# Delta-rule recurrence on one core: the leaf decays on GpSimd, the last leaf written into the compact array, and WL's product ahead of the identity's

## What is computed

```python
def step(S, t):
    q_t, k_t, v_t, a_t, b_t = t
    y = jnp.einsum('bhvk,bhk->bhv', S, k_t)
    err = y - v_t
    S = a_t[..., None] * S - (b_t[..., None] * err)[..., None] * k_t[:, :, None, :]
    o = jnp.einsum('bhvk,bhk->bhv', S, q_t)
    return (S, o)
```

## Time and profile before

| | |
|---|---|
| median of 3 runs | 3173.81 us (3172.24 to 3183.9) |
| profiled execution | 3174.62 us, of which the span 3172.8 us |
| TensorE busy | 2838.1 us, 89% |
| VectorE busy | 2322.8 us, 73% |
| ScalarE busy | 1605.5 us, 51% |
| GpSimd busy | 1317.6 us, 42% |
| granted TensorE clock, mean | 0.977 of full speed |

### The profile page before, as it was taken

How to read it: one execution, slowest core, us unless ns; L and a number is a source line. 1 busy time by engine, 2 the same in 40 slices (tenths; PEclk the granted TensorE clock), 3 DMA queues, 4 the chain that set the end, 5 groups by cost and what they waited for, 6 DMA issues and landing times. The chain is left out here.

```text
span 3172.8 us, 48588 instructions
## 1 busy us (share of the span) xinstructions
PE 2838.1 (89%) x14144; PEld 2012.0 (63%) x14144; DVE 2322.8 (73%) x4837; ACT 1605.5 (51%) x3516; POOL 1317.6 (42%) x1574
## 2 busy tenths in 40 slices
PE   7999999678898898988989898898888989869999
PEld 3555555366676776666766676776767767645555
DVE  6777777578888778887787878788887788724332
ACT  6666666445555555554554555555555555421111
POOL 3666767624443444443443434444334444310000
PEclk9999999889999999999999999999999999979999
DMA  3655565631222322222323222322223222034220
GB/s 133 242 202 231 234 241 202 225 60 34 54 42 41 60 51 54 43 41 42 69 41 55 41 42 43 67 46 51 42 41 65 46 54 42 8 105 89 55 44 14
DMA packets 449884, 261.23 MB, mean 82 GB/s; under 512 B 402672, under 2 KB 414672, under 8 KB 447472
## 3 DMA queue, kind: packets, MB, share of 16 engines
q1 hardware_dynamic: 449664, 258.51, 31.5%
HBM read 153.42 MB, written 105.05 MB: 81 GB/s over the span
## 5 line engine op out<-in xcount | busy, mean ns | idle before, releaser
L265 DVE SCALAR_TENSOR_TENSOR A_acc<-A_psY,A_w,A_acc 128x410 f32<-128x410 f32 (+1 forms) x720 | 419.2, 637 | 151.6 <-ACT A_acc L334 151.6
L1155 ACT ACTIVATE B_WL<-B_psT 64x128 f32<-64x128 f32 (+3 forms) x480 | 148.6, 310 | 512.4 <-PE B_psT L1576 512.4
L840 POOL TENSOR_TENSOR B_WT<-B_WT,B_G 128x128 f32<-128x128 f32 (+2 forms) x224 | 183.0, 817 | 513.0 <-PE B_psT L1576 493.3
L405 PE MATMUL A_psY<-A_xT,A_w 128*128 128x413 f32 (+1 forms) x960 | 347.2, 510 | 9.1 <-PE A_psAG L411 7.7
L192 POOL TENSOR_TENSOR A_outs<-A_outs,A_acc 128x410 f32<-128x410 f32 (+1 forms) x240 | 229.7, 987 | 215.5 <-ACT A_outs L342 215.5
L1068 DVE TENSOR_TENSOR B_NC<-B_NC,B_psM 128x256 f32<-128x256 f32 x480 | 199.1, 415 | 143.9 <-PE B_psM L1603 101.8
L405 PEld LDWEIGHTS A_psY<-A_xT,A_w 128*128 128x128 f32 x960 | 180.2, 189 | 165.5 <-issue 164.2
L822 POOL TENSOR_TENSOR B_PQ<-B_PQ,B_G 128x256 f32<-128x256 f32 x128 | 125.8, 983 | 368.3 <-DVE B_WT L1036 368.3
L1071 DVE TENSOR_REDUCE B_W<-B_NC 128x64 f32<-128x320 f32 x512 | 248.7, 486 | 17.6
L1603 PE MATMUL B_psM<-B_BD,B_WL 128*128 128x128 f32 x1536 | 237.6, 296 | 12.6
L334 ACT ACTIVATE A_acc<-A_psY,A_w 128x410 f32<-128x410 f32 (+1 forms) x240 | 166.2, 692 | 162.9 <-PE A_psY L405 161.2
(11 more groups left out here) (197 smaller groups left out, 6703.5 us busy)
## 6 DMA issues: line engine op xcount, KB each, us to landing
B_KQ<-scr SPq DMA_DIRECT2D x96, 512.0 KB, 6.8
scr<-A_outs SPq DMA_DIRECT2D x48, 615.0 KB, 3.5
scr<-A_outag SPq DMA_DIRECT2D x32, 615.0 KB, 5.2
scr<-A_outs SPq DMA_DIRECT2D x48, 409.0 KB, 2.5
A_xc<-nbeta SPq DMA_DIRECT2D x16, 1024.0 KB, 5.9
B_A<-scr SPq DMA_DIRECT2D x32, 512.0 KB, 5.0
B_C<-scr SPq DMA_DIRECT2D x32, 512.0 KB, 5.9
B_G<-scr SPq DMA_DIRECT2D x32, 512.0 KB, 4.6
```

The lines of the kernel that those rows point to most:

```text
L265: nc.vector.scalar_tensor_tensor(a, y, w[:, s, col:col + 1], a, ALU.mult, ALU.add)\
L405: last = nc.tensor.matmul(psY[p][:, y0:y0 + HALO + t1 - t0], wp[:, p, kt, :], xT[:, kt, t0:t1 + HALO], start=kt == 0, stop=kt == KT - 1)
L840: tt(dst, dst, gr, ALU.mult).then_inc(wsc.sem, 1)
L1155: copy = lambda out, in_: nc.scalar.activation(out, in_, ACT.Copy)
```

## The change

Three edits, all in the recurrence.

1. In leaves 3, 7 and 11 VectorE writes the decayed W of the last leaf into its place in WC instead of WT. TensorE waits for the first copy alone. ScalarE copies that leaf from WC back to WT after the WL copy, and `scale_left` on GpSimd waits for this.
2. The decays of chunk g + 1 are six GpSimd products of one row each (`row_decays`, 128x256), spread over leaves 2 to 9: part 0 after the first two gates, part 1 in leaf 4, part 2 after leaf 6's right scaling, part 3 after leaf 7's left scaling, parts 4 and 5 in leaves 8 and 9. `dec` counts 6 instead of 3. Chunk 0's stay on VectorE.
3. In even leaves but leaf 0 TensorE issues the WL product first (`start=True`) and the identity product second.

```diff
-DEC = 3
+DEC = 6
...
+            def row_decays(g, *parts):
+
+                a, e = by_leaf_row(A[:, g % 2]), E[:, g % 2]
+                products = ((RR_, a[:, 1], a[:, 2]), (B_, e[:, RR_], a[:, 3]), (F_ + 1, a[:, 0], a[:, 1]),
+                            (B_ + 1, a[:, 2], a[:, 3]), (F_ + 2, e[:, F_ + 1], a[:, 2]), (F_ + 3, e[:, F_ + 2], a[:, 3]))
+                for k in parts:
+                    row, x, y = products[k]
+                    if k == 0:
+                        loaded(pool, "A", g)
+                        wait(pool, nc0, 2 * g - 3, 5)
+                    else:
+                        wait(pool, dec, g, {1: 1, 4: 3, 5: 5}.get(k, 0))
+                    tt(e[:, row], x, y, ALU.mult).then_inc(dec.sem, 1)
...
                 wait(pool, tps, g, j + 1)
+                if p >= 2:
+                    wait(pool, wc, g, {3: 2, 7: 4, 11: 6}[j])
...
                 gates(0, 1)
+                rows(0)
                 past(g, 3)
...
                 gates(3)
+                rows(1)
                 past(g, 5)
...
                 scale_right(g, 7, (1,))
+                rows(2)
                 past(g, 7)
                 scale_left(g, 7)
+                rows(3)
                 past(g, 8)
                 scale_right(g, 9)
+                rows(4)
                 past(g, 9)
                 scale_left(g, 9)
+                rows(5)
                 scale_right(g, 11)
...
-                    tt(WT[:, j] if j % 2 else WR[:], W[:, :, lf], E[:, g % 2, B_:B_ + R, :, j].rearrange("p r h -> p h r"), ALU.mult).then_inc(wt.sem, 1)
+                    p, n, _ = merge_of(j)
+                    if j < JM and p >= 2:
+                        to = WC[:, 0:H * n].rearrange("p (h t) -> p h t", h=H)[:, :, n - R:n]
+                    else:
+                        to = WT[:, j] if j % 2 else WR[:]
+                    tt(to, W[:, :, lf], E[:, g % 2, B_:B_ + R, :, j].rearrange("p r h -> p h r"), ALU.mult).then_inc(wt.sem, 1)
...
-                    elif j == 8 and more:
-                        decays(g + 1, (0,))
...
-                            decays(g + 1, (1,))
...
-                            wait(act, wt, g, j + 1)
-                            left_compact(g, j, (j,))
                         wait(act, tps, g, j + 1)
                         wait(act, mps, g, 2 * j)
...
                         copy(WL[0:rows_, 0:w_], psT[0:rows_, 0:w_]).then_inc(wl.sem, 1)
+                        if p >= 2:
+                            wait(act, wt, g, j + 1)
+                            copy(WT[:, j], WC[:, 0:H * n].rearrange("p (h t) -> p h t", h=H)[:, :, n - R:n]).then_inc(wc.sem, 1)
...
-                            wait(pe, wc, g, {3: 2, 7: 4, 11: 6}[j])
+                            wait(pe, wc, g, {3: 1, 7: 3, 11: 5}[j])
...
-                            wait(pe, psc0, g, pair_number(j) + 1)
-                            mm(psM[:, 0:2 * rs], ident[:], pair(g)[:, :, :, r0:r0 + n], start=True, stop=False)
-                            wait(pe, wl, g, j + 1)
-                            mm(psM[:, 0:2 * rs], WL[0:rs, 0:128], OWN[0:rs, j // 2, :, :, R:2 * R],
-                               start=False, stop=True).then_inc(mps.sem, 2)
+                            if j:
+                                wait(pe, wl, g, j + 1)
+                                mm(psM[:, 0:2 * rs], WL[0:rs, 0:128], OWN[0:rs, j // 2, :, :, R:2 * R], start=True, stop=False)
+                                wait(pe, psc0, g, pair_number(j) + 1)
+                                mm(psM[:, 0:2 * rs], ident[:], pair(g)[:, :, :, r0:r0 + n],
+                                   start=False, stop=True).then_inc(mps.sem, 2)
```

More of the change, by code:

```diff
@@ L578, in recurrence @@
         kl, kc = Count(sem("leaf_keys"), 2), Count(sem("block_keys"), 3)
-        wc = Count(sem("left_compact"), 6)
+        wc = Count(sem("left_rearranged"), 6)
         wec = Count(sem("w_end"), 2)
@@ L852, in _ @@
                 queries(1)
+                rows = lambda *parts: row_decays(g + 1, *parts) if g + 1 < NCH else None
                 past(g, 2)
                 gates(0, 1)
+                rows(0)
                 past(g, 3)
@@ L904, in _, with first_decays @@
             wait(dve, zeros, 0, NZERO)
[L906 to L921, removed]
+            def first_decays():
+                loaded(dve, "A", 0)
+                wait(dve, dcp, 0, 2)
+                a, e = by_leaf_row(A[:, 0]), E[:, 0]
+                tt(e[:, F_ + 1:B_ + 2:3], a[:, 0:3], a[:, 1:4], ALU.mult).then_inc(dec.sem, 3)
+                wait(dve, dec, 0, 3)
+                tt(e[:, F_ + 2:B_ + 1:4], e[:, F_ + 1:RR_ + 1:3], a[:, 2:4], ALU.mult).then_inc(dec.sem, 2)
+                wait(dve, dec, 0, 5)
+                tt(e[:, F_ + 3], e[:, F_ + 2], a[:, 3], ALU.mult).then_inc(dec.sem, 1)
             def coefs(h):
@@ L1134, in chunk @@
                     add_state(g, i)
-            decays(0)
+            first_decays()
             nc.vector.memset(NC[:, 1], 0.0).then_inc(zeros.sem, 1)
@@ L1341, in chunk @@
                         p, n, r0 = merge_of(j)
-                        if p >= 2:
-                            wait(act, wt, g, j + 1)
-                            left_compact(g, j, (j,))
                         wait(act, tps, g, j + 1)
@@ L1584, in chunk @@
                             wait(pe, ow, g, 2 if j < 8 else 4)
-                            wait(pe, psc0, g, pair_number(j) + 1)
-                            mm(psM[:, 0:2 * rs], ident[:], pair(g)[:, :, :, r0:r0 + n], start=True, stop=False)
-                            wait(pe, wl, g, j + 1)
-                            mm(psM[:, 0:2 * rs], WL[0:rs, 0:128], OWN[0:rs, j // 2, :, :, R:2 * R],
-                               start=False, stop=True).then_inc(mps.sem, 2)
+                            if j:
[4 more added lines that the diff above has]
+                                   start=False, stop=True).then_inc(mps.sem, 2)
+                            else:
+                                wait(pe, psc0, g, 1)
+                                mm(psM[:, 0:2 * rs], ident[:], pair(g)[:, :, :, r0:r0 + n], start=True, stop=False)
+                                wait(pe, wl, g, 1)
+                                mm(psM[:, 0:2 * rs], WL[0:rs, 0:128], OWN[0:rs, 0, :, :, R:2 * R],
+                                   start=False, stop=True).then_inc(mps.sem, 2)
                         else:
```

## The result

The changed kernel takes 3118.65 us (median of 4 runs, 3117.38 to 3120.34) against 3174.42 for the one before (4 runs): ratio 0.9819, interval 0.9804 to 0.9834. I had predicted 3177, with 3140 to 3200 as the range. The profiled execution took 3120.34 us.

A forecast was written before the change was run, and what follows sets the result against it. VectorE and TensorE were taken to end the recurrence's leaves in turn. Gains and costs nearly cancelled, +0.1 us a chunk, +3 us over 31 chunks: 3177 us as a median, range 3140 to 3200.

The forecast's parts named there:

- The ring: Each leaf's loop through VectorE, TensorE and ScalarE back to VectorE; VectorE and TensorE were said to take turns ending it.
- Decays onto GpSimd: Six 128x256 products, 6.0 us on GpSimd, covered there; VectorE sheds 3.42 us a chunk but waits in collisions.
- I take 0.80 us each, 1.6 us: Leaves 6 and 7: parts 2 and 3 each delay a VectorE solution step by 0.80 us, bounded by 0 and 1.13.
- Rival C: Leaves 6 and 7: a full block, parts 2 and 3 costing 1.13 us each, 3197 us; chance 0.07.
- Leaf 10's transposition comes forward by its idle 1.11 us and no more: Leaf 10 on TensorE: VectorE's relief gains only the 1.11 us idle there, 1.1 us a chunk if nothing else happens.
- Part 5 against the decayed W: Leaf 10: part 5 pushes two scalings onto the decayed W, 0.4 us of VectorE, hidden on TensorE's side.
- Part 0 at leaf 3 and part 4 at leaf 9: Each can hold up that leaf's decayed W on VectorE while TensorE is still busy; counted as 0.
- The compact route: Leaves 3, 7, 11: ScalarE's copy leaves the way, gaining 0.24 us at leaf 3, 0.33 at 11, nothing at 7.
- The later left scaling: GpSimd's left scaling comes about 0.5 us later, with no user for several leaves; 0.5 cost if that cover were gone.
- The swap: WL product first in even leaves: costs 0.39 us at leaves 4 and 12, gains up to 0.35 at leaf 8.
- rival B: Slower by the product order: TensorE also ends leaves 2 and 6, 0.78 us a chunk more, 3201 us; chance 0.17.
- A: Parts 2 and 3 slip into VectorE's gaps and the relief is gained: -1.1 us a chunk, 3140 us; chance 0.36.

The follow-up runs named there:

- compact_only: The kernel before with only the last leaf (3, 7, 11) written straight into the compact array: 3155.75 us, ratio 0.9927.
- decays_only: The kernel before with only the next chunk's decays moved from VectorE to GpSimd: 3158.79 us, ratio 0.9923.
- no_swap: The changed kernel with the old order, identity product ahead of the WL product: 3140.84 us, ratio 0.9889 against the kernel before.
- swap_only: The kernel before with only the WL product put ahead of the identity product in even leaves but leaf 0: 3217.35 us, ratio 1.0126.
- row2_moved: The changed kernel with decay row product 2 made right after row product 1, away from leaf 6's solution steps: 3107.77 us, ratio 0.9796 against the kernel before.
- fill_before: The kernel before with leaf 9's second decay transposes issued three times to fill TensorE's idle time, same output: 3189.95 us, ratio 1.005.
- fill_before_swap14: The kernel before with leaf 9's second decay transposes issued three times and the WL product first in leaf 14 alone: 3159.43 us, ratio 0.9942.

## Why the prediction was wrong, step by step

The ring, leaf by leaf: by how much the stretch between two products grew against the kernel before, as the sum had it and as even chunks show it (medians of chunks 2 to 30), in us.

| from product of leaf | predicted | measured | off by |
|---|---|---|---|
| 0 to 6 | +0.15 | -0.03 | -0.18 |
| 6 to 7 | +0.80 | +0.36 | -0.44 |
| 7 to 8 | +0.80 | +0.43 | -0.37 |
| 8 to 9 | -0.91 | -0.80 | +0.11 |
| 9 to 10 | -1.14 | -1.56 | -0.42 |
| 10 to 11 | +0.40 | +0.17 | -0.23 |
| 11 to 12 | -0.30 | -0.30 | 0 |
| 12 to 14 | +0.40 | +0.25 | -0.15 |
| 14 to the next chunk | -0.20 | +0.01 | +0.21 |
| sum | 0 | -1.47 | -1.47 |

**Decays onto GpSimd: the mechanism right, the term mis-sized.** The step that failed is "I take 0.80 us each, 1.6 us". The products met the two solution steps named. Leaf 7's product came 0.36 later, leaf 8's another 0.43, 0.79 together, and of this the decays are 0.71: `compact_only`, which moves no decays, already shows 0.07 at leaf 8. There were two reasons. The rows are cheaper than 1.13: parts 2 and 3 took 0.91 and 1.04 us even while contended (part 2 alone 0.68). The nearest row that I took, 1.13, has another access pattern; the six parts come in two kinds, 0.66 us with both inputs from A and 0.86 with one from E, when they meet nothing. And the price was carried over from products that begin under a VectorE instruction in full course. Part 2 starts at 1512.33 while the step before it (1511.41 for 1.42 us) is nearly through; the step it holds up appears at 1512.68, when the product has 0.56 us left to its end at 1513.24, and it lost 0.40. Part 3 had 0.49 left when the last step of leaf 7 appeared at 1518.44, which lost 0.35. In both, then, the loss was a little less than what was left of the GpSimd product when the step appeared (that the rest at that moment is what counts is my reading of these two cases). The second collision made leaf 8's product late, but not the leaf: TensorE was busy until about 1520.6 and stood still 0.1 us before the transposition of 1520.72. This is read from the rows; no run moved part 3 alone.

Put right by the 0.81 us of the two rows in the table, the sum would have been about 3153 us, inside the range. It took the next step and the clock as well to bring the result below it.

The Trainium skill's page "SBUF — State Buffer" (section "SBUF: two separate sides") describes the shared port pair as an exclusive lock held for the whole instruction, with the loser fully blocked. The runs agree on the exclusion: the step took 1.27 us with part 2 beside it and 0.87 without. By a lock over the whole instruction a loser waits at most the winner's length; here it waited 0.40 of 0.91 us, since 0.35 of them were over when it began. Rival C, which priced the full block, had no support.

**"Leaf 10's transposition comes forward by its idle 1.11 us and no more": true, and not the bound.** Counted from leaf 0's product it came forward 1.01 us in the odd chunks shown (from 38.20 to 37.19) and 1.13 in the medians. The product of leaf 11 came forward more, 1.30 and 1.42, because TensorE had not been what ended that leaf. Two engines' timelines of the kernel before:

```profile
1554.13 0.49 PE L1588 MATMUL B_psM<-B_OWN,B_WL 64*128 64x128 f32 x2
```

```profile
1552.73 0.27 DVE L1073 TENSOR_TENSOR B_WR<-B_W,B_E 128x64 f32<-128x64 f32 x1
...
1553.30 0.29 DVE L1031 TENSOR_TENSOR B_PQ<-B_PQ,B_E 128x128 f32<-128x128 f32 x1
...
1554.25 1.27 DVE L1012 TENSOR_TENSOR B_ST<-B_ST,B_ring 128x512 f32<-128x512 f32 x2
...
1555.44 0.41 DVE L1068 TENSOR_TENSOR B_NC<-B_NC,B_psM 128x256 f32<-128x256 f32 x1
```

The merged term was there at 1554.62, and the product waited 0.8 us more for VectorE's own queue. VectorE had no idle time from leaf 9 to leaf 11, and in the changed kernel none from leaf 10's product to leaf 11's. So leaf 11's product follows leaf 10's, which came forward 1.61, less 0.19 that part 5 adds. I had read TensorE's idle time before its own instruction as the limit, where the question was which engine releases the next product last. A smaller part of the same step: I let leaf 10's product wait for the modelled end of the matmuls before it, while it starts 0.19 us ahead of that end (1525.16 against 1524.64 + 0.71).

**Part 5 against the decayed W.** Predicted 0.4 us of VectorE, hidden behind TensorE. L1095 took 0.37 instead of 0.27 and the scaling behind it, L1048, 0.36 instead of 0.29. With the small shifts between them that makes 0.19, and it is not hidden: VectorE releases leaf 11's product, which is 0.18 further from leaf 10's in `decays_only` too. Part 0 at leaf 3 and part 4 at leaf 9 cost nothing, as put.

**The compact route.** By `no_swap` against `decays_only`: 0.25 gained at leaf 4 (predicted 0.24), nothing gained at leaf 7, as put, and 0.3 at leaf 12 (0.3). The swap in the changed kernel cancels the first. The later left scaling, which I had put at nothing, cost 0.07: it now meets a step of leaf 7's solution that takes 1.50 us instead of 1.43, in `compact_only` as well.

**The swap.** By the changed kernel against `no_swap`: leaf 5 is 0.42 later (predicted 0.39), of which 0.19 comes back before leaf 6's product, where I had carried all of it on; between leaves 8 and 9 it gains 0.33 (predicted up to 0.35); between 9 and 10 another 0.20, not predicted; between 12 and 13 it loses 0.25 (predicted 0.39). Net nothing. In `swap_only` it costs 0.5 a chunk and eleven more half-clock stretches: rival B's direction with a smaller price per chunk, and the clock on top.

**The clock was not in the sum.** I compared the lengths of two chunks and took the even one for typical; every few even chunks took 67 us. Their clock was one view away. It was worth 15 us of the change's 54 (of which the tail took some 6 back), and about 20 us between two versions that the sum could not have told apart.

**The rivals.** A (relief cashed, -1.1 a chunk, 3140 us) was the closest, with a chance of 0.36: its end is what happened from leaf 10 on. Its reason, that the products slip into gaps, is not. Even A's full gain lacked 0.35 us a chunk and the clock, so the range's lower end, set by A, lay 21 us too high. I had given the unsized terms no room on the side of a gain.

## What to carry to other kernels

Before work is moved off an engine, ask of each leaf or iteration which engine releases its next step last, and follow the relief along that engine until another one is last; idle time elsewhere on the ring is not the limit by itself. In both collisions timed here the price was at most the time from the victim's request to the other's end, so place both instructions before pricing one. Look at the granted TensorE clock of many iterations before calling one typical, and test small edits by time as well as by schedule, since the order of two products was worth 0.7 to 1% here, nearly all of it through the clock.

## What the runs showed of the hardware

- A float32 product of 128x256 on GpSimd took 0.65 to 0.68 us with both inputs from A and nothing beside it (part 2, `row2_moved`), 0.86 with one input from E (parts 1, 4 and 5), and 0.91 and 1.04 with both from A beside a VectorE product of operands in SBUF (parts 2 and 3, changed kernel). The VectorE step beside it lost 0.40 and 0.35 us.
- In a recurrence in which TensorE is busy 88 to 90% of the time, its granted clock fell to 1.2 GHz for stretches of 3 to 14 us, in or just after leaves in which it is idle for 1.25 to 1.55 us in all; each cost 0.6 to 5.8 us. Filling the idle time at leaf 10 moved the stretches to leaves 14 and 15 (`fill_before`), and only with the order of two products changed there did they go (`fill_before_swap14`), with the same idle time. Fewer and shorter idle times do not by themselves mean less time at half clock.
- The part after the last chunk's first product, unchanged in all kernels, took 446 us before and 452 after, with 50 and 59 us at half clock in it.
